# Attention on one core: whole-block value matmuls, the maxima unit at the head of each half step, output tiles in the maxima banks

## The reference

```
xn = layernorm(x)
q, kv = xn @ Wq, xn @ Wkv              # 16 heads of 16, both rotated by the rotary table, q also scaled by 1/4
attn = softmax(q kv^T) kv              # 64 head-batches, 1024 x 1024 scores each
ffn = (silu(xn Wg^T) * (xn Wu^T)) Wd^T # int weights / 127, hidden 768
out = x + attn @ Wout + bout + ffn
```

## Time and profile before

| what | value |
|---|---|
| median of 3 runs | 915.94 us (913.67 to 917.18) |
| profiled execution, own time | 918.31 us |
| its span | 916.4 us |
| PE busy | 847.3 us, 92% of the span |
| DVE busy | 763.9 us, 83% |
| ACT busy | 695.1 us, 76% |
| POOL busy | 187.2 us, 20% |
| mean granted clock of TensorE | 0.986 |

### The profile page before, as it was taken

The page is one execution under the profiler, slowest core; times in us unless marked ns, Lnnn a source line. Parts: engine busy times, 40 slices in busy tenths (PEclk is TensorE's granted clock), DMA queues, the critical chain, the costliest instruction groups (busy, mean ns, idle before and its releaser), DMA issues.

```text
span 916.4 us, 18500 instructions
## 1 busy us (share of the span) xinstructions
PE 847.3 (92%) x7018; PEld 319.0 (35%) x7018; DVE 763.9 (83%) x932; ACT 695.1 (76%) x1317; POOL 187.2 (20%) x411
## 2 busy tenths in 40 slices
PE   2999999999799999999999999999999999999798
PEld 1455565564322222222222223222222222222234
DVE  5787776698989999999999999988999998999502
ACT  4354655523389999999998999898989999998583
POOL 4333444433300010000111111111211111121020
PEclk9999999999989999999999999999999999999799
DMA  9012111011001111111111122111111221111222
GB/s 328 18 47 73 55 47 46 31 64 46 19 19 30 27 26 26 39 30 32 37 43 49 44 59 55 49 43 42 43 49 51 57 53 46 43 44 48 65 69 78
DMA packets 58494, 47.39 MB, mean 52 GB/s; under 512 B 18189, under 2 KB 48717, under 8 KB 58405
## 3 DMA queue, kind: packets, MB, share of 16 engines
q1 hardware_dynamic: 58404, 46.20, 17.8%
HBM read 28.57 MB, written 16.90 MB: 50 GB/s over the span
## 4 chain that ended last, share of the span: by engine, by line
PE 64%; DVE 17%; ACT 10%; issue 5%; DMA 2%; SPq 1%; POOL 0%; DVEq 0%; ACTq 0%
PE ps L677 22%; PE ps L694 11%; PE ps L660 11%; DVE negmax L1147 10%; ACT arena L946 7%; PE ps L574 6%; PE ps L536 4%; PE ps L603 4%; PE ps L702 3%; DMA arena<-inv_d 1%; DVE side L1053 1%; DVE stats L1005 1%; PE ps L589 1%; DMA x_all<-x_dram 1%; DVE arena L1040 1%
## 5 line engine op out<-in xcount | busy, mean ns | idle before, releaser
L1147 DVE TENSOR_REDUCE negmax<-ps 128x2 f32<-128x1024 f32 x512 | 594.3, 1216 | 53.5 <-PE ps L694 53.2
L946 ACT ACTIVATE arena<-ps 128x512 f32<-128x512 f32 x1024 | 555.8, 597 | 61.2 <-PE ps L660 39.9
L677 PE MATMUL ps<-arena 128*32 128x256 f32 (+1 forms) x3664 | 317.7, 419 | 0.3 <-ACT arena L946 0.2
L660 PE MATMUL ps<-qs,ks 51*128 51x512 f16 x1024 | 200.2, 386 | 24.3 <-ACT arena L946 23.4
L694 PE MATMUL ps<-ks,qs 48*128 48x512 f16 x1024 | 200.0, 388 | 7.8 <-DVE negmax L1147 7.7
L694 PEld LDWEIGHTS ps<-ks,qs 48*128 48x128 f16 x1024 | 49.1, 93 | 184.3 <-issue 147.6
L677 PEld LDWEIGHTS ps<-arena 128*32 128x32 f32 x3664 | 72.6, 108 | 115.4 <-issue 101.9
L660 PEld LDWEIGHTS ps<-qs,ks 51*128 51x128 f16 x1024 | 50.9, 93 | 138.7 <-ACT arena L946 109.1
L574 PE MATMUL ps<-arena,side 128*128 128x512 f16 x384 | 88.1, 384 | 6.8 <-DVE side L1053 5.9
L1281 POOL TENSOR_TENSOR side<-side 128x512 f16<-128x512 f32 x48 | 55.8, 1165 | 75.8 <-ACT side L880 75.8
L874 ACT ACTIVATE side<-ps 128x512 f32<-128x512 f32 x48 | 28.5, 593 | 55.9 <-PE ps L574 55.9
(11 more groups left out here) (78 smaller groups left out, 456.3 us busy)
## 6 DMA issues: line engine op xcount, KB each, us to landing
parts_d<-arena SPq DMA_DIRECT2D x64, 128.0 KB
x_all<-x_dram SPq DMA_DIRECT2D x8, 512.0 KB, 8.0
qs<-parts_d SPq DMA_DIRECT2D x64, 64.0 KB, 1.9
ks<-parts_d SPq DMA_DIRECT2D x64, 64.0 KB, 1.9
o_d<-arena SPq DMA_DIRECT2D x124, 32.0 KB
arena<-o_d SPq DMA_DIRECT2D x24, 128.0 KB
arena<-inv_d SPq DMA_DIRECT2D x48, 64.0 KB
out_dram<-arena SPq DMA_DIRECT2D x24, 128.0 KB, 1.8
```

The lines of the kernel that those rows point to most:

```text
L660: mm = pe.matmul(ps[:, score_bank(ls, 2 * half + a), :], ks[ring][top:top + ROWS, kt * P:(kt + 1) * P], qs[ring][top:top + ROWS, half * CH ...
L677: mm = pe.matmul(ps[32 * j:32 * j + 32, 7, cols], vstage[pl % 2][:, j % 2, kt, :], probs[PER_STEP * (kt % PBUF) + j][:, cols], start=(kt = ...
L946: act.activation(probs[PER_STEP * (kt % PBUF) + j], ps[:, score_bank(ls, j), :], ACT.Exp).then_inc(exp_done, 1)
L1147: dve.tensor_reduce(negmax[pl % 2][:, h, :, kt], ps[:, 2 * h:2 * h + 2, :], AX.X, ALU.max, negate=True).then_inc(max_done, 1)
```

## The change

1. The value tables and the half blocks go. A whole block of values (four matmuls of 512 columns) stands in every even slot, at slot 2 kt + 4 (slots 16 and 18 are slots 0 and 2 of the next pair); odd slots have none.
2. The maxima unit is the first thing on PE in every half step, ahead of the scores. Before, it came after the values, or between scores and a long block.
3. `turn_max` moves from the end of slot 12 to slot 13, ahead of the scores.
4. The output tile moves from slot 3 to slot 7 of its pair, behind the maxima unit and ahead of the scores. It goes to the banks of the maxima unit that would come next (`max_slot`, `tile_bank`), not to bank 7, and DVE adds x from there (`add_tile`); the ACT copy and the POOL add are gone. The late tiles move from slots 3, 6, 11 of pair 31 to 5, 9, 11.
5. `copy_o` comes after the second exp of step 1 of a pair, not after the first.

Its core:

```diff
-TILE_SLOT = 3
+TILE_SLOT = 7
+TURN_SLOT = 2 * T_AT + 1
-TILE_VALUES = {5: (0, WHOLE), 6: (1, 0), 7: (1, 1), 8: (2, 0), ...
-PLAIN_VALUES = {4: (0, 0), 5: (0, 1), 6: (1, 0), 7: (1, 1), 8: (2, 0), ...
+VALUES = {2 * kt + 4: kt for kt in range(STEPS)}
+TILE_UNIT = MAXES * LAG + 2 * LEAD + TILE_SLOT
-LATE_AT = {6: 22, 11: 23}
+LATE_AT = {5: 21, 9: 22, 11: 23}
+        def tiles_ahead(n):
+            return min(max((n - TILE_UNIT - 1) // MAXES + 1, 0), LOOP_TILES)
+        def max_slot(n):
+            return (n + tiles_ahead(n)) % 2
+        def tile_bank(n):
+            return 2 * (1 - max_slot(TILE_UNIT + MAXES * n)) if n < LOOP_TILES else 0
...
                 for half in range(2):
                     slot = 2 * (ls % STEPS) + half
-                    scores(turn, ls, half, not last_turn or pl + 1 < RING)
...
-                    if more and long:
-                        maxima(turn, m, half)
-                    if tile and slot == TILE_SLOT:
-                        pe.wait_ge(o_copied, p)
-                        project_tile(*tile, 7)
-                    if block:
-                        values(of, pair, *block, tile)
+                    if MAXES * p + 2 * LEAD + slot < MAXES * PAIRS:
+                        maxima(turn, ls + LEAD, half)
+                    if slot == TILE_SLOT and LAG <= p < LAG + LOOP_TILES:
+                        project_tile(p - LAG)
+                    if slot == TURN_SLOT and not final:
+                        turn_max(p + 1, pl + 1, PER_STEP * (STEPS * p + T_AT))
+                    scores(turn, ls, half, not final)
+                    if slot in VALUES:
+                        values(p, pl, VALUES[slot])
+                    elif p and slot + 2 * STEPS in VALUES:
+                        values(p - 1, pl - 1, VALUES[slot + 2 * STEPS])
...
-                    if more and not long:
-                        maxima(turn, m, half)
...
-                    if j == 0 and kt == COPY_O_AT and not (isinstance(p, int) and p == 0):
-                        copy_o(p - 1, ls // STEPS - 1, turn)
+                    if j == 1 and kt == COPY_O_AT and p:
+                        copy_o(p - 1, pl - 1, turn)
...
+            def add_tile(n):
+                dve.wait_ge(wout_done, CREDIT + n + 1)
+                dve.wait_ge(res_free[n % 2], 16 * (n // 2 + 1))
+                dve.tensor_tensor(res[n % 2], ps[:, tile_bank(n), 0:DIM], x_all[:, n, :], ALU.add).then_inc(res_done, 1)
```

More of the change, by code:

```diff
@@ L662, in scores, with values @@
                 mm.then_inc(scores_done, 1)
-            def values(p, pl, kt, part, tile=None):
+            def values(p, pl, kt):
                 if kt == 0:
@@ L668, in values @@
                     pe.wait_ge(o_copied, p)
[L669 to L674, removed]
-                for j in range(PER_STEP):
[L677 to L681, removed]
+                pe.wait_ge(exp_done, PER_STEP * (STEPS * p + kt + 1))
+                for j in range(PER_STEP):
+                    mm = pe.matmul(ps[32 * j:32 * j + 32, 7, :], vstage[pl % 2][:, j % 2, kt, :],
+                                   probs[PER_STEP * (kt % PBUF) + j], start=(kt == 0), stop=(kt == STEPS - 1))
+                mm.then_inc(pv_done, 1)
             def maxima(turn, m, h):
@@ L718, in project_back, with step @@
                           start=False, stop=False)
-            def step(turn, ls, last_turn=False, tile=None):
+            def step(turn, ls):
                 pl = ls // STEPS
                 p = turn * RING + pl
-                m = ls + LEAD
-                more = not last_turn or m < RING * STEPS
+                final = p + 1 == PAIRS
                 for half in range(2):
                     slot = 2 * (ls % STEPS) + half
-                    scores(turn, ls, half, not last_turn or pl + 1 < RING)
[L729 to L733, removed]
-                    if more and long:
-                        maxima(turn, m, half)
-                    if tile and slot == TILE_SLOT:
-                        pe.wait_ge(o_copied, p)
-                        project_tile(*tile, 7)
-                    if block:
-                        values(of, pair, *block, tile)
-                    if last_turn and pl + 1 == RING:
+                    if MAXES * p + 2 * LEAD + slot < MAXES * PAIRS:
[9 more added lines that the diff above has]
+                        values(p - 1, pl - 1, VALUES[slot + 2 * STEPS])
+                    if final:
                         if slot == 0:
@@ L801, in _ @@
             pe.wait_ge(y_done, CT * NCHUNK)
[L802 to L814, removed]
+            for p in range(PAIRS):
+                for kt in range(STEPS):
+                    step(p // RING, p % RING * STEPS + kt)
+            for slot in range(2 * STEPS, 2 * STEPS + 4):
+                if slot in VALUES:
+                    values(PAIRS - 1, RING - 1, VALUES[slot])
             pe.wait_ge(back_divided, CPB)
@@ L933, in _, with exps @@
             high(d, KH - 1)
-            def exps(turn, ls, tile=None, last_turn=False):
-                p = turn * RING + ls // STEPS
+            def exps(turn, ls):
+                pl = ls // STEPS
+                p = turn * RING + pl
                 kt = ls % STEPS
@@ L947, in exps @@
                                    ).then_inc(exp_done, 1)
-                    if j == 0 and kt == COPY_O_AT and not (isinstance(p, int) and p == 0):
-                        copy_o(p - 1, ls // STEPS - 1, turn)
[L950 to L953, removed]
+                    if j == 1 and kt == COPY_O_AT and p:
+                        copy_o(p - 1, pl - 1, turn)
+                    if j == 1 and kt == T_AT and p + 1 < PAIRS:
+                        rows(p + 1, pl + 1, turn)
             def copy_o(p, slot, turn):
@@ L1365, in slot @@
                     divide(*tile)
-                for tile in tiles:
-                    if not isinstance(tile[0], int) or tile[0] < LOOP_TILES:
-                        add_tile(*tile, tile[0])
                 q = j + 1
@@ L1387, in _ @@
                 slot(TURNS, j, [(n, n % 2)])
-            for n in range(LOOP_TILES, (BATCH - 1) * BT):
+            for n in range(PAIRS - LAG, TILES):
                 divide(n, n % 2)
```

79 lines of the change are left out of this document (26 added, 53 removed).

## The result

The changed kernel takes 977.16 us (median of 4 runs, 976.85 to 979.9) against 915.64 us before (median of 4 runs, 913.67 to 917.18): ratio 1.068, 95% interval 1.0652 to 1.0708, a loss of 61.5 us. The forecast was 969 (955 to 985), a loss of 53. The profiled execution has a span of 975.0 us against 916.4.

What follows compares the result with a forecast made beforehand. PE's list and the PE-ACT loop through three score banks were taken to bound half steps side by side at 1.1 us. Start 2.8, plain pairs 14.9, tile pairs 42.2, end -6.9 gave +53.0: 969 us (955 to 985).

Steps and rivals of the forecast that it cites:

- The step of 2.62 us: Two half steps of the loop: scores 1.54 and 1.08 apart by turns, 2.62 us a step against 2.43 before.
- The plain pair: Pair of heads without output tile: eight steps plus 0.16 for the turn, 21.12 us, +1.65; nine intervals, +14.9 us.
- the second rival: Every step: scores released after 1.17 instead of 1.08, +22 us, 991 us in all; chance 0.06.
- The tile: Output tile ahead of the odd scores: +1.16 us, tile pair 22.28, +2.11; twenty intervals, +42.2 us.
- a copy that is not hidden: copy_o behind the second exp: expected to be hidden before the odd exp; if not, 0.2 us a pair.
- The end: From the last loop copy on: 50.6 us falls to 43.2, -7.4, entered as -6.9 with 0.5 counted at the start.
- The start: Up to the first copy: first scores +1.35 us, seven steps at +0.21, later copy half a microsecond; together +2.8.
- One sign: DVE's idle time was to grow by 2 us a pair, released by the maxima line.
- The first: Whole loop: the ring does not bind, plain pairs 18.7 us, tile pairs 19.1, kernel faster at 880 us; chance 0.07.
- the ring: PE-ACT loop through three score banks: scores wait for the half step before's first exp, no half step under 1.08 to 1.09.
- The clock (third): Clock falls to 1.2 GHz in the loop because PE rests 0.47 in each 2.62; some 1074 us; chance 0.04.
- The absorbed tile (fourth): Output tile in the tile pairs costs nothing, 20 x -1.16 us, 946 us; chance 0.02.

Runs made afterwards that it cites:

- x1: Changed kernel with the third of a step's four exps (first of the odd half step) cut to half its columns: 928.02 us.
- x2: Changed kernel with the first of a step's four exps (first of the even half step) cut to half its columns: 977.89 us.
- x3: Changed kernel with the value blocks back in halves, all else as changed: 919.95 us.
- x6: Kernel before with whole value blocks in every other slot of pairs 0 to 9, all else as before: 941.24 us.
- x7: Kernel before with the maxima unit first in every half step, all else as before: 911.75 us.
- x8: Changed kernel with the second wait of the scores of slots 14 and 0 moved ahead of the maxima unit: 972.95 us.
- x4: Changed kernel with the output tile behind the scores of slot 7 instead of ahead of them: 968.4 us.

## Why the prediction was right

**The step of 2.62 us** was right to 0.01: 1.55 and 1.07 to 1.08 in the trace, ACT's idle 0.39 (0.40 read beforehand), PE's wait 0.47 (forecast 0.5). What carried it was one existing whole block in the trace of before and the scores without values in the earlier trace rows: the new loop is those two intervals laid end to end. Experiments x1 and x2 show that it is the loop through the first odd exp, x3 and x6 that the whole blocks make it, x7 that the order does not.

**The plain pair** was forecast at 21.12 and is 21.41, 9 intervals +17.5 us instead of +14.9. The missing 0.29 are two terms. In front of slots 14 and 0 the scores have two waits and take 1.17, not 1.08: 0.18 (x8 took 0.17 of it away). I had seen the 1.17 in the earlier trace rows and made it a rival for every step, where it belongs to two of sixteen half steps. This is also what became of the second rival (a slower release everywhere, 991 us): in front of the other even slots the release came at 1.07 to 1.08. And from unit to turn PE takes 0.32 (373.92 to 374.24 in the trace), where I took unit to scores, 0.22, as the nearest row: 0.10. The margin of the range, 0.04 a step, was meant for the step, which needed none of it; the error came from these two terms, 0.036 a step.

```profile
373.92 0.39 PE L689 MATMUL ps<-ks,qs 48*128 48x512 f16 x2
...
374.24 0.23 PE L640 MATMUL ps<-identh,mparts 128*128 128x128 f16 x1
```

**The tile** costs 1.16 to 1.17 in a pair, as forecast: 20 intervals +48.2 instead of +42.2, of which 5.8 are the 0.29 of every pair. Its places on PE and its bank gave no wait:

```profile
585.96 0.39 PE L689 MATMUL ps<-ks,qs 48*128 48x512 f16 x2
586.28 1.13 PE L701 MATMUL ps<-wo,arena 128*128 128x256 f32 x4
...
587.34 0.39 PE L659 MATMUL ps<-qs,ks 51*128 51x512 f16 x2
...
588.43 0.39 PE L659 MATMUL ps<-qs,ks 51*128 51x512 f16 x2 [0.27 <-ACT arena L931]
```

DVE's add is hidden, and so is the copy behind the second exp; x6 shows what it costs where it is not moved, 0.69 a pair; my price for a copy that is not hidden was 0.2.

**The end** gave 7.8 back (50.6 to 42.8), 7.4 in my sum. The wait of 6.13 in front of pair 30's tile is gone altogether and the clock stayed up.

**The start** was +2.8 in the sum. The words there do not add up: seven steps at 0.21 are 1.5 by themselves, and with the half microsecond of the later copy the first copy would come 3.3 later. The total of 53.0 is not touched, because the half microsecond was left out here and again at the end (6.9 in place of 7.4), and the two cancel. The first copy is at 275.3 instead of 274.7, but the part in front of the loop, which the change does not touch, was 2.7 us shorter in this execution (its last feed-forward matmuls start at 244.00, those of before at 246.69). So the term is about +3.3. The profiled execution before took 918.31 us, 2.7 above its median, which would account for the spans differing by 58.6 where the medians differ by 61.5.

Added up: 53.0 + 2.6 (plain pairs) + 6.0 (tile pairs) - 0.4 (end) = 61.2, against 61.5 measured.

**One sign** came out smaller than forecast: DVE's idle time in front of the reductions grew from 53.5 to 90.4 us, 1.2 a pair instead of 2. The others came as written, with the copies 0.3 further apart.

**The rivals.** The first (the ring does not bind, 880 us) fell. Its ground was that PE loses work, and that is so: a whole block takes 1.00 to what follows (365.06 to 366.06) where two halves took twice 0.57, and PE's busy time fell from 847.3 to 818.6 us. The Trainium skill, TensorEngine Tiling (Array Packing), Tiling Modes, states that changing the tiling mode drains TensorE. The trace agrees as far as one block costs less than two halves; no run separates the drain from other costs of a group. That saving is worth nothing while the ring sets the pace: x3 gives it up again and is 57 us faster. The clock (third) did not fall in the loop behind pair 0; in pair 0 it stood at the 1.2 GHz level for 6.8 us, as before. The absorbed tile (fourth) did not happen ahead of the scores, and behind them 0.44 of its 1.16 us were absorbed (x4).

## What to carry to other kernels

With a short ring of buffers between two engines, each stretch of work between two hand-overs counts by itself, and a short one cannot lend its spare time to a long one (1.54 and 1.08 here, though PE's own work in a step had fallen from 2.22 to 1.98). The same work is free where the producer waits for the ring and costs in full where the consumer waits for the producer. Before merging small pieces into big ones, look in the trace for one place where a big one already stands, and measure the distance across it. And put a bulky extra (a tile, a copy) in the slot whose neighbours are empty: here 0.24 us instead of 1.16 for the same instructions.

## What the runs showed of the hardware

- Work taken from an engine inside a loop is worth its full time or nothing, by which instruction it is: half the columns of one exp in four (0.38 us instead of 0.60) are worth 49 us when it is the third, nothing when it is the first (x1, x2).
- Scores that wait for two semaphores started 0.09 us later after the release than with the same second wait passed earlier (1.18 and 1.08 in the comparison of x8). The load of their weights started 0.11 us after the end of the exp instead of 0.05.
- Where PE goes from a group of 48 or 51 rows of fp16 to one of 128 rows, the starts were 0.32 apart (scores to values 375.79 to 376.11, unit to tile 510.73 to 511.05, unit to turn 373.92 to 374.24), against 0.22 from unit to scores (375.57 to 375.79); the next time I would take 0.32 for every such pair that a trace does not hold.
- In pair 0 the granted clock stood at the 1.2 GHz level for 6.8 us in the kernels before and after and 13.7 us in x6. The gaps before it were alike in the first two. I do not know what lengthened it in x6.
